# The experts' second layer as three one-pass products of 12-bit parts, its weights split during the attention

## What is computed

```python
eid = jnp.argmax(x @ centroids.T, axis=-1)          # one expert for each token
xln = xn * ln_g[eid] + ln_b[eid]                    # xn: x normalised
for e in range(8):
    h = jax.nn.relu(xln @ w1[e] + b1[e])            # first layer, 256 -> 1024
    ffn += onehot[:, e:e+1] * (h @ w2[e] + b2[e])   # second layer, 1024 -> 256
out = layernorm(x + alpha * ffn)
```

## Time and profile before

| | |
|---|---|
| median of three executions | 1427.6 us |
| profiled execution: its own time, its span | 1430.41 us, 1428.6 us |
| TensorE's mean granted clock | 0.98 of 2.4 GHz |
| busy over the span: PE, PEld | 1372.3 us (96%), 846.4 us (59%) |
| busy over the span: DVE, ACT, POOL | 1071.4 (75%), 870.2 (61%), 258.4 us (18%) |
| first `hide` starts, last result row is made | 1134.9 us, 1425.7 us |
| DMA | 134.08 MB, mean 94 GB/s |

### The profile page before, as it was taken

The page is one execution under the profiler, slowest core; times in us unless marked ns, Lnnn a source line. Parts: engine busy times, 40 slices in busy tenths (PEclk is TensorE's granted clock), DMA queues, the critical chain, the costliest instruction groups (busy, mean ns, idle before and its releaser), DMA issues. The chain is left out here.

```text
span 1428.6 us, 44125 instructions
## 1 busy us (share of the span) xinstructions
PE 1372.3 (96%) x18460; PEld 846.4 (59%) x18460; DVE 1071.4 (75%) x2004; ACT 870.2 (61%) x1775; POOL 258.4 (18%) x388
## 2 busy tenths in 40 slices
PE   7999999999999999999999999899987699999998
PEld 4554344444444444444444444788776589999997
DVE  2567888988888888889888880555788576777666
ACT  3445668778787787787877877655455333333342
POOL 4332011102110111021111110000345411111111
PEclk9999999999999999999999999999998599999999
DMA  7685311212212211122300000314424544445441
GB/s 222 212 209 122 73 25 37 46 30 50 48 33 46 45 36 46 31 51 46 93 3 3 3 3 2 118 43 161 172 74 151 201 181 178 175 181 183 167 180 73
DMA packets 77824, 134.08 MB, mean 94 GB/s; under 512 B 12226, under 2 KB 64443, under 8 KB 72252
## 3 DMA queue, kind: packets, MB, share of 16 engines
q1 hardware_dynamic: 59612, 108.84, 25.8%
q10 hardware_dynamic: 14608, 14.00, 3.0%
q0 software_dynamic: 3408, 8.43, 1.7%
HBM read 67.75 MB, written 23.11 MB: 64 GB/s over the span
## 5 line engine op out<-in xcount | busy, mean ns | idle before, releaser
L1799 DVE TENSOR_REDUCE part_max<-pair 128x2 f32<-128x1024 f32 (+2 forms) x576 | 643.2, 1161 | 73.5 <-PE pair L1216 44.4
L1611 ACT ACTIVATE big<-pair 128x512 f32<-128x512 f32 (+1 forms) x1120 | 584.9, 598 | 185.4 <-PE pair L1244 176.2
L1244 PE MATMUL pair<-big 128*32 128x512 bf16 (+3 forms) x5120 | 345.1, 349 | 3.9 <-DMA big<-max_t 3.3
L1216 PE MATMUL pair<-big 128*32 128x512 bf16 (+3 forms) x5120 | 340.7, 349 | 4.9 <-DVE part_max L1799 4.5
L1266 PE MATMUL pair<-big 128*17 128x512 f32 (+3 forms) x2560 | 288.0, 528 | 0.7 <-POOL big L2228 0.3
L1216 PEld LDWEIGHTS pair<-big 128*32 128x32 bf16 x5120 | 125.1, 96 | 185.5 <-DVE part_max L1799 87.1
L1244 PEld LDWEIGHTS pair<-big 128*32 128x32 bf16 x5120 | 123.2, 96 | 158.1 <-ACT big L1611 71.6
L1624 ACT ACTIVATE std<-moments,eps_col 128x1 f32<-128x1 f32 (+1 forms) x110 | 32.5, 295 | 220.8 <-DVE moments L1837 211.3
L1502 PE MATMUL pair<-big,tok 128*128 128x128 f32 x1248 | 148.1, 278 | 7.2 <-DVE big L2112 7.2
L1502 PEld LDWEIGHTS pair<-big,tok 128*128 128x128 f32 x1248 | 147.2, 194 | 10.2 <-DVE big L2112 8.3
L1514 PE MATMUL pair<-big 128*128 x624 | 141.0, 379 | 0.0
(11 more groups left out here) (184 smaller groups left out, 1285.2 us busy)
## 6 DMA issues: line engine op xcount, KB each, us to landing
tok<-big SPq DMA_DIRECT2D x39, 1024.0 KB
big<-in_L_ffn_w SPq DMA_DIRECT2D x16, 1024.0 KB
big<-split_dram SPq DMA_DIRECT2D x216, 64.0 KB, 2.8
split_dram<-big ACTq DMA_DIRECT2D x32, 384.0 KB, 4.0
big<-split_dram SPq DMA_DIRECT2D x42, 256.0 KB, 4.2
big<-routed_dram SPq DMA_DIRECT2D x39, 129.0 KB, 2.1
tok<-in_L_attn_x SPq DMA_DIRECT2D x8, 512.0 KB, 6.7
big<-in_c_query_rows SPq DMA_DIRECT2D x8, 512.0 KB, 4.9
```

The source lines that it names most:

```text
L1216: mm = pe.matmul(bank[q:q + STRIPE, o:o + w], m.q_op[slot][:, step.qt, h, step.r * P + q:step.r * P + q + STRIPE], m.k_op[slot][:, h, step ...
L1244: mm = pe.matmul(m.bank[step.bank][k:k + STRIPE, n * w:(n + 1) * w], m.k_op[slot][:, h, step.kb * P + k:step.kb * P + k + STRIPE], m.q_op[ ...
L1611: act.activation(m.p_ring[:, step.place, step.heads[0]:step.heads[-1] + 1, step.at:step.at + w], m.bank[step.bank][:, 0:len(step.heads) * ...
L1799: dve.tensor_reduce(m.part_max[(step.u * QT + step.qt) % 2][:, step.r, step.heads[0]:step.heads[0] + n, step.c], banks[:, :, 0:w], X, ALU. ...
```

## The change

`w2` is no longer loaded as it is. Three parts change:

1. **In the attention**, for each expert e: SP loads `w2[e]` (1 MB) into `tok`'s second half; DVE makes the high part in four pieces (128x512 each, the low 12 bits masked off by a bitwise and on int32); POOL subtracts it from the whole to get the low part, in four pieces; SP stores both parts (2 MB) to `w2_dram`. These steps are put into the front's list by score number: load at 140 + 54 e, pieces at +16, +20, +24, +28, store at +36.
2. **In the back**, the same 16 loads of 1 MB as before now fetch the low and high parts of `w2`; `w1` stays in DRAM. In the experts each tile's `w1` is read from DRAM instead of copied within SBUF.
3. **In the experts**, the hidden values are split alike. `hidden_t` and the low part exist once instead of twice; the high part twice. `unhide` becomes 24 one-pass products (float32r) of 128x128 by 128x256: high by high, high by low, low by high.

```diff
+WEIGHTS_FROM, WEIGHTS_EVERY = 140, 54
+    def split_weights(self):
+        while self.weights and self.weights[0][0] <= self.n_score:
+            step = self.weights.pop(0)[1]
+            self.steps.append(step)
+            if isinstance(step, SplitWeights):
+                self.dve += 400
+                self.pool = max(self.pool, self.dve + self.LAG) + 1160
...
 def unhide(i):
-        pe.wait_ge(s.rect_act, i + 1)
-        pe.wait_ge(s.rect_dve, i + 1)
+        pe.wait_ge(s.high_set, 2 * i + 2)
         for f in range(FC):
-            mm = pe.matmul(m.bank[b][:, 0:D], m.hidden_t[i % 2][:, f, :],
-                           m.w2[:, bass.ds(e, 1), f, :].rearrange("p a n -> p (a n)"),
-                           start=(f == 0), stop=(f == FC - 1))
+            for part in (HIGH, LOW):
+                pe.matmul(m.bank[b][:, 0:D], m.hidden_high[:, i % 2, f, :],
+                          m.w2[:, part, bass.ds(e, 1), f, :].rearrange("p a n -> p (a n)"),
+                          start=(f == 0 and part == HIGH), stop=False)
+        pe.wait_ge(s.low_set, 2 * i + 2)
+        for f in range(FC):
+            mm = pe.matmul(m.bank[b][:, 0:D], m.hidden_low[:, f, :],
+                           m.w2[:, HIGH, bass.ds(e, 1), f, :].rearrange("p a n -> p (a n)"),
+                           start=False, stop=(f == FC - 1))
...
 (ACT, rectify)
+        if i == 0:
+            act.wait_ge(s.scatter[2], 16 * SCATTERS)
+            act.wait_ge(s.scatter[3], 16 * SCATTERS)
+        else:
+            act.wait_ge(s.low_set, 2 * i - 1)
         act.wait_ge(s.hidden, 2 * i + 1)
...
         done.then_inc(s.rect_act, 1)
+        for half in range(2):
+            act.wait_ge(s.masked, 2 * i + half + 1)
+            act.activation(m.hidden_high[:, i % 2, half * FC // 2:(half + 1) * FC // 2, :], m.high_bits[half],
+                           ACTF.Copy).then_inc(s.high_set, 1)
...
 (DVE, front)
+        elif isinstance(step, SplitWeights):
+            dve.wait_ge(s.w2_in, 16 * (step.e + 1))
+            dve.tensor_scalar(m.weight_piece(HIGH, step.n).bitcast(I32), m.weight_piece(LOW, step.n).bitcast(I32),
+                              -(1 << LOW_BITS), None, ALU.bitwise_and).then_inc(s.w2_high, 1)
...
 (DVE, experts)
+    def split(i, half):
+        f = slice(half * FC // 2, (half + 1) * FC // 2)
+        if i:
+            dve.wait_ge(s.high_set, 2 * i - 1 + half)
+            dve.wait_ge(s.low_set, 2 * i - 1 + half)
+        dve.tensor_scalar(m.high_bits[half].bitcast(I32), m.hidden_t[:, f, :].bitcast(I32), -(1 << LOW_BITS), None,
+                          ALU.bitwise_and).then_inc(s.masked, 1)
 def rectify(i):
+        dve.wait_ge(s.rect_act, i + 1)
+        split(i, 0)
+        if i:
+            dve.wait_ge(s.low_set, 2 * i)
         dve.wait_ge(s.hidden, 2 * i + 2)
...
         done.then_inc(s.rect_dve, 1)
+        dve.wait_ge(s.rect_dve, i + 1)
+        split(i, 1)
...
 def pool_experts(nc, m, s):
+    def rest(i):
+        if i:
+            pool.wait_ge(s.unhidden, i)
+        for half in range(2):
+            f = slice(half * FC // 2, (half + 1) * FC // 2)
+            pool.wait_ge(s.masked, 2 * i + half + 1)
+            pool.tensor_tensor(m.hidden_low[:, f, :], m.hidden_t[:, f, :], m.high_bits[half], ALU.subtract).then_inc(s.low_set, 1)
+    rest(0)
     for i in range(SLOT_TILES):
+        if i + 1 < SLOT_TILES:
+            rest(i + 1)
         pool.wait_ge(s.final_set, i + 1)
...
 (SP, front)
+        elif isinstance(step, LoadWeights):
+            if step.e == 0:
+                sp.wait_ge(s.x_turned, 2 * TILES)
+            else:
+                sp.wait_ge(s.w2_out, 16 * step.e)
+            sp.dma_start(m.tok[:, BPB:BPB + FC, 0:D],
+                         t["L1_ffn_w2"][step.e].rearrange("(c p) n -> p c n", p=P)).then_inc(s.w2_in, 16)
+        elif isinstance(step, StoreWeights):
+            sp.wait_ge(s.w2_low, PIECES * (step.e + 1))
+            sp.dma_start(m.w2_dram[step.e].rearrange("p a c n -> p (a c) n"),
+                         m.tok[:, BPB:BPB + 2 * FC, 0:D]).then_inc(s.w2_out, 16)
...
 (SP, experts, fetch_w1)
-        sp.dma_start(m.w1_now[k][:, :, :].rearrange("p c f -> p (c f)"),
-                     m.w1[:, bass.ds(e, 1), :, :].rearrange("p a c f -> p (a c f)")).then_inc(s.w1_in[k], 16)
+        sp.dma_start(m.w1_now[k][:, :, :],
+                     w1_rows[bass.ds(e, 1), :, :].rearrange("a (c p) f -> p (a c) f", p=P)).then_inc(s.w1_in[k], 16)
```

More of the change, by code:

```diff
@@ L66 @@
 EARLY = (AT_X - W_BYTES) * EXPERTS // W_BYTES
+AT_HIDDEN, AT_LOW = AT_V + 10304, W1_AHEAD * KC * FF * 4
+LOW_BITS = 12
+LOW, HIGH = 0, 1
+PIECES, PIECE = 4, 2
+WEIGHTS_FROM, WEIGHTS_EVERY = 140, 54
 SCORE_BANKS, SUMS_BANK, MAX_BANKS = (0, 1, 2), 3, ((4, 5), (6, 7), (0, 1))
@@ L97 @@
 Residuals = namedtuple("Residuals", "ring")
+LoadWeights = namedtuple("LoadWeights", "e")
+SplitWeights = namedtuple("SplitWeights", "e n")
+StoreWeights = namedtuple("StoreWeights", "e")
 def max_pieces(u):
@@ L167, in __init__ @@
         self.to_issue, self.fold_at, self.fold_ring = [], None, 0
+        self.weights = []
+        for e in range(EXPERTS):
+            at = WEIGHTS_FROM + e * WEIGHTS_EVERY
+            self.weights += [(at, LoadWeights(e))] + [(at + 16 + 4 * n, SplitWeights(e, n)) for n in range(PIECES)]
+            self.weights += [(at + 36, StoreWeights(e))]
     def room_at(self):
@@ L902, in __init__, with early @@
         self.t = t
+        with ExitStack() as first:
+            def early(name, shape, dt=F32R):
+                return first.enter_context(nc.sbuf_tensor(name, shape, dt))
+            self.w2 = early("w2", [P, 2, EXPERTS, FC, D])
+            early("before_high", [P, (AT_HIDDEN - 2 * W_BYTES) // 4], F32)
+            self.hidden_high = early("hidden_high", [P, 2, FC, P])
+            early("before_low", [P, (BIG - AT_HIDDEN + AT_LOW) // 4 - 2 * FC * P], F32)
+            self.hidden_low = early("hidden_low", [P, FC, P])
         self.big = big = sb("big", [P, BIG // 4])
@@ L1012, in __init__ @@
         self.count_all = self.bank[ALL_BANK][:, 0:EXPERTS]
-        self.final_f = [carve(AT_V + 23640 + i * 1280, [40, EXPERTS], parts=1) for i in range(2)]
+        self.final_f = [carve(AT_V + 23656 + i * 1280, [40, EXPERTS], parts=1) for i in range(2)]
         self.used = self.spectral_bias[0:1, :].rearrange("p (a b) -> p a b", a=EXPERTS)
@@ L1030, in __init__ @@
         at = AT_V
-        self.xs = [carve(AT_V + at, [ROW]) for at in (18480, 19512, 20544, 4096, 5128, 21576)]
+        self.xs = [carve(AT_V + at, [ROW]) for at in (18496, 19528, 20560, 4096, 5128, 21592)]
         self.mixed = [carve(AT_V + i * 1024, [D]) for i in range(2)]
@@ L1036, in __init__ @@
         self.xln_t = [carve(at + 2048 + i * 1024, [KC, P]) for i in range(2)]
-        self.hidden_t = [carve(at + 4096 + i * 4096, [FC, P]) for i in range(2)]
         tok_flat = self.tok[:, :, :].rearrange("p b n -> p (b n)")
+        self.hidden_t = tok_flat[:, AT_LOW // 4 + FC * P:AT_LOW // 4 + 2 * FC * P].rearrange("p (c n) -> p c n", c=FC)
+        self.high_bits = [self.acc_t[half][:, :].rearrange("p (c n) -> p c n", c=FC // 2) for half in range(2)]
         self.w1_now = [tok_flat[:, i * KC * FF:(i + 1) * KC * FF].rearrange("p (c f) -> p c f", c=KC)
@@ L1041, in __init__, with weight_piece @@
         self.gate = self.recip_l[:, :, :].rearrange("p a b -> p (a b)")
+    def weight_piece(self, part, n):
+        at = BPB + (part == HIGH) * FC + n * PIECE
+        return self.tok[:, at:at + PIECE, 0:D]
     def group(self, g):
@@ L1111, in __init__ @@
         self.xn_set, self.tile_turned, self.xln_set = sem("xn_set"), sem("tile_turned"), sem("xln_set")
+        self.w2_in, self.w2_high, self.w2_low, self.w2_out = sem("w2_in"), sem("w2_high"), sem("w2_low"), sem("w2_out")
+        self.masked, self.high_set, self.low_set = sem("masked"), sem("high_set"), sem("low_set")
         self.hidden, self.rect_act, self.rect_dve = sem("hidden"), sem("rect_act"), sem("rect_dve")
@@ L2131, in rectify @@
             f = FC // 2 + j
-            done = dve.tensor_scalar(m.hidden_t[i % 2][:, f, :], m.bank[b][:, j * P:(j + 1) * P],
+            done = dve.tensor_scalar(m.hidden_t[:, f, :], m.bank[b][:, j * P:(j + 1) * P],
                                      col[:, f, bass.ds(e, 1)], 0.0, ALU.add, ALU.max)
         done.then_inc(s.rect_dve, 1)
+        dve.wait_ge(s.rect_dve, i + 1)
+        split(i, 1)
     def finish(i):
@@ L2417, in sync_back @@
         elif isinstance(step, Experts) and step.early:
-            for e in range(EXPERTS):
-                sp.dma_start(m.w1[:, e, :, :],
-                             t["L1_ffn_w1"][e].rearrange("(c p) f -> p c f", p=P)).then_inc(s.experts_in, 16)
-            for e in range(EARLY):
-                sp.dma_start(m.w2[:, e, :, :], w2_view[:, e, :, :]).then_inc(s.experts_in, 16)
+            for part, experts in ((LOW, EXPERTS), (HIGH, EARLY)):
+                for e in range(experts):
```

(1 more changed line is left out.)

20 lines of the change are left out of this document (13 added, 7 removed).

## The result

The changed kernel takes 1486.57 us (median of four executions, 1485.07 to 1488.15), the kernel before 1427.97 beside it: a ratio of 1.0408, 95% interval 1.0393 to 1.0423. The forecast was 1477 (1449 to 1512). The profiled execution took 1488.15 us, its span is 1486.3.

What follows compares the result with a forecast made beforehand. TensorE was taken as the bound, VectorE within 3%, then VectorE after the change. 1428.6 + 46.2 (masks 39.8, table loads 15.0, slack -8.6) + 3 for the attention gave a 1477.8 us span; forecast 1477, range 1449 to 1512.

Steps and rivals of the forecast that it cites:

- PE gains 0.82 us: Experts, TensorE: 24 one-pass products replace the 16 records of `unhide`, so a tile needs 6.43 us, 0.82 less.
- Slack 0.22: Experts, VectorE: of the 0.88 us gap ahead of L2112, only 0.22 us a tile is real slack.
- Masks 1.02: Experts, VectorE: two masks a tile of 0.41 us each, with handovers and lost overlap, add 1.02 us a tile.
- the rival of one element a cycle: Experts, VectorE: masks run at one element a cycle, 0.68 us each, giving 1499 us; chance 18%.
- POOL's hold, 0.05 or less: Experts: POOL's subtractions hold VectorE's operations by 0.05 us or less a tile, with nothing in the sum.
- named in the rival: Experts: VectorE is held by POOL once a tile, giving 1500 us; chance 8%.
- Table load 0.42: Experts, ACT: the square root's table loads behind the second copy, 1.25 us more every third turn, 0.42 a tile.
- The sum: Experts: VectorE takes 8.49 us a tile after the change; over the 39 tiles this adds 46.2 us.
- Attention +3: Attention: one row of maxima is caught behind weight transfers on SP's queue, 3 us; bounds 0 and 15.
- The start, counted alike: Start of the experts: its lists run on VectorE's chain too, so they were counted like the tiles.
- ACT's new wait for the scatters, costed at 0: Start of the experts: POOL has issued all scatters before ACT's first rectify, so the wait costs 0.
- The rival of a falling clock: Experts, TensorE: idle time lowers its clock; at a steady 1.2 GHz it needs 12.9 us a tile, over 1600; chance 4%.

Runs made afterwards that it cites:

- experiment 2: The kernel before with two masks on VectorE added for each tile, written to a buffer nobody reads: ratio 1.0158 to the kernel before.
- experiment 3: The changed kernel with GpSimd's two subtractions of a tile cut to 4 of each 128 columns from the second tile on: ratio 1.0308 to the kernel before.
- experiment 1: The changed kernel with its one-pass products but no masks, copies or subtractions in the experts: ratio 0.9959 to the kernel before.
- experiments 4 and 7: The changed kernel with a square root issued early (1.0327); or, in the attention, no weight splitting (1.0336), weights on ScalarE's queue (1.0456), stores in pieces (1.0388).
- experiment 8: The changed kernel without masks, rectifying operations moved from VectorE to ScalarE: two of four 1.0180, all four 1.0062, the last version 0.9994 of the kernel before.

## Why the prediction was right, and which terms were off

The bound moved to VectorE, by the masks and the late table load, as forecast. Several terms were off, and they cancel.

- **PE gains 0.82 us.** Of this only VectorE's slack would show: right in kind. The gain is 7.18 - 6.59 = 0.59. The old tile was counted as 7.27 from 33 operations in 240 us, and worked out as 7.25, where the first and last row give 7.18. The new pace is 6.59, not 6.43, since a one-pass product with its weights takes 0.120 us and not the 0.110 of the transpose in the earlier trace rows (0.24 more for 24); `hide` and the transposes took 0.08 less than was counted.
- **Slack 0.22.** Mis-sized: 7.18 - 6.80 = 0.38 at least. The step that failed is that 0.66 of the gap ahead of `turn` was taken as VectorE's own in every turn. In the changed kernel, where VectorE doesn't wait for PE, the gap is 0.41 or 0.42 us in 15 of the 24 turns from 1200 to 1400 us, 0.66 or 0.67 in 7, and longer in two; in the mean it is 14.5 / 28 = 0.52. The 0.41 that the earlier trace rows showed once was the usual case. This made the forecast 0.16 x 39 = 6 us too high.
- **Masks 1.02.** Measured 0.93 when POOL does nothing (experiment 2), with 0.42 us for each, and the rival of one element a cycle (0.68) fell.
- **POOL's hold, 0.05 or less.** This failed, as named in the rival: the price is 0.37 us a tile (experiment 3), 14 us in all. The step put POOL's first subtraction wholly under the four rectifying operations; it starts 0.4 us after the first of them, is 1.28 us long, not 1.16, and so reaches 0.56 us into the second mask. By the rule of the Trainium skill (SBUF: State Buffer, section "Who interferes with whom") that VectorE's tensor_scalar in a two-port mode shares the port pair with GpSimd, the runs agree: 0.42 to 0.84, and 0.41 to 1.20 us.
- **Table load 0.42.** The mechanism was right: 1.75 against 0.36 us is 1.39 in each third turn. Taking it away gave 0.27 a tile; of the missing 0.19, 0.07 came back as longer holds, and the rest is open.
- **The sum.** 6.80 + 0.93 + 0.37 + 0.27 = 8.37 us, and the tile takes 8.40. From the first to the last result row the change costs 319.0 - 272.8 = 46.2 us, the very number of the forecast (for all 39 tiles, the start's among them), but this is luck. Against the forecast, the hold that was left out adds 0.37 us a tile, and the slack that was too small (0.16) and the masks and table load that were too dear (0.09 and 0.15) take away 0.40.
- **Attention +3.** Measured +6.9, and 5.1 to 10.5 between any two traces with the one and the other attention. The mechanism was the one named, rows of maxima caught by a store, once, 2.9 us. What wasn't in the step is that the engines fall out of step behind it: ACT waited 4.55 us.
- **The start, counted alike.** From the first `hide` to the first result row it takes 23.9 us in place of 17.5, and this 6.4 was missing. Counted from the second `hide`, the row comes after 10.4 us in the kernel before and with the products alone (experiment 1), 11.7 with masks added to the kernel before (2), 13.2 with short subtractions (3), 15.3 in each of the four traces with the changed kernel's instructions in this stretch (experiments 4 and 7), and 17.0 in the changed kernel. Three things are in it:
  - ACT's new wait for the scatters, costed at 0, makes 1.7 us. ACT's first rectifying operation comes 8.4 us after the first `hide` starts and not 5.5, and 6.3 us after POOL issued the last scatter. The label in the changed kernel is "issue" (first row below), but the trace of the version of experiment 8 with two operations moved, which keeps this wait, names it (second). In three of the four traces above ACT waits for PE there instead, since the scatters are over, and in the fourth the wait ends before the second `hide` starts.
  - POOL's subtractions make 2.1 us. They also hold two small operations with which VectorE chooses the rows (last rows), and which take 0.19 and 0.17 us in the kernel before.
  - The masks and the copies behind them make the other 2.8 us, of which the masks alone are 1.3 by experiment 2. The first tiles have no other tile behind which these could hide; for the remaining 1.5 us this is argued, not shown.

```profile
1148.43 1.14 ACT L1763 ACTIVATE tok<-pair,columns 128x128 f32<-128x128 f32 x4 [2.89 <-issue]
```

```profile
1149.05 0.63 ACT L1765 ACTIVATE tok<-pair,columns 128x128 f32<-128x128 f32 x2 [1.86 <-DMA routed_dram<-tok,position]
```

```profile
1159.35 2.50 POOL L2354 TENSOR_TENSOR hidden_low<-tok,acc_t 128x512 fp32r<-128x512 f32 x2 [6.34 <-PE pair L1557]
1159.86 0.82 DVE L2151 TENSOR_TENSOR spectral<-spectral 1x40 f32<-1x40 f32 x1
1160.70 1.18 DVE L2152 TENSOR_SCALAR tile_row<-spectral 1x37 int32<-1x37 f32 x1
```

- **The clock.** The rival of a falling clock did not come: the granted clock is 0.95 in the experts. It does fall for a moment: in six of the eight gates' turns from 1200 to 1400 us, after PE was idle for 2.2 to 2.6 us, one `hide` takes 5.35 to 5.47 us and not 3.84, and the granted clock is 0.50 (1.2 GHz) from 1291 to 1294 us, in the turn shown above. VectorE, which sets the pace, does not wait for it.

The profiled span is 8.5 us above the forecast's 1477.8: 3.9 from the attention and 6.4 from the start, less 1.7 between them, a difference that the spread of that stretch covers. The median, 9.6 us above the forecast, lies 0.3 above this span, where the forecast took 1 below.

## What to carry to other kernels

Where two engines are within a few per cent of each other, price a change on the second one first, and measure its slack with a run that takes the first one's work away; a label "issue" ahead of an operation doesn't tell whose time it is. Work moved to GpSimd is not free because GpSimd is idle: look at which VectorE operations with only SBUF operands will run at the same time, and put it under those that read PSUM. Such an operation can wait out one GpSimd instruction or two, so every reordering has to be followed by a look at the mean duration of each VectorE line. And the first turn of a loop has to be priced by itself: what other tiles hide later stands in the open there.

## What the runs showed of the hardware

- A VectorE tensor_scalar with a bitwise operation on int32, SBUF to SBUF, takes 0.42 us for 128x512: near the 0.41 that the prediction worked out for two elements a cycle, and not the 0.68 for one. Beside a GpSimd tensor_tensor of 1.28 us it took 0.84, and an fp32 one of 128x256 (0.41 alone) took 1.20.
- With two such GpSimd instructions in a row, VectorE's operation was held through both in one version (0.41 became 2.24 us) and let through after the first in another (1.19 us). Which of the two happens was not explained.
- A scalar_tensor_tensor with both inputs in SBUF is held alike (0.49 to 1.05 us); one input in PSUM and it isn't (0.41 at 1278.94, inside GpSimd's second subtraction).
- One-pass products of float32r operands, 128x128 by 128x256 with a fresh weight load each, start 0.120 us apart, where the fp32 product took two records that start 0.216 us apart.
- 4 KB rows that are issued while a 2 MB store is under way come late whether they stand on the store's queue (PE waited 2.9 us for them) or on another (2.6); with stores of 256 KB the longest wait was 0.9.
